# One group-scan kernel: the stack of high and low rows built by DMAs from SBUF to SBUF instead of by TensorE transposes, with the job table placed anew

## The chip, the cores and the metric

The kernel runs on one core of one Trainium2 chip. The metric is the device time of one execution in microseconds, taken as the median of several runs; lower is better. TensorE is called PE here, VectorE DVE, ScalarE ACT, GpSimd POOL, SyncE SP.

## The reference

The input is 32 sequences of 64 tokens with 1024 channels, all in fp32. Two adapted layers are applied with residuals:

```
u  = x W + (x A[id1]) B[id1]                      # per sequence a LoRA pair, rank 16
xp = u xproj^T -> dt_in (32), B (16), C (16)
dt = softplus(dt_in dtproj^T + b)
h_t = exp(dt A) * h_{t-1} + dt * u * B_t          # 1024 channels x 16 states, 64 steps
x1 = x + sum_n h_t[n] C_t[n] + D * u
h2 = x1 W2^T + bias + lora2[id2](x1)              # folded into the router and expert product
out = x1 + sum_e gate_e(h2) * 4 * (h2 A_e^T) B_e^T    # top 2 of 4 experts, softmax over them
```

## The kernel before, in words

The work is cut into 8 groups (`GROUPS`) of 4 sequences, T = 256 tokens. A group is run as 8 steps j, one for each 128 channels, and a step as 4 units (`UNITS`): unit `un` is half = un // 2 of the 16 states and p = un % 2 of the tokens. There are 256 units in all. A unit is a pipeline over four engines. PE computes `dBx` = B * dt * u in PSUM by 4 matmuls with 96 contraction rows (`b_times_dtx`); DVE scans it with the decays `dA` that ACT has made (8 ACTIVATEs a half step, `decays`); POOL multiplies the states by `Cb` into `hC`; and three units later PE sums the 8 states by accumulating transposes into a bank `yp` (`sum_states`), to which `Du` = D * u is added.

The 96 rows of `dBx`'s weights are the diagonals `Bd` (32 tokens by 32, three times: high, high and low part of B) and its moving operand is `stacked`: for each of the 8 blocks of 32 tokens, the high, the low and again the high part of dtx = dt * u, with tokens on the partitions. In the kernel before it is made in five steps for each j: POOL makes `dtx` (channels on partitions, `make_dtx`), ACT rounds it and writes it twice into `HL` (`make_high`), POOL subtracts (`make_low`), PE transposes 8 blocks 128 x 96 into PSUM in two jobs named `stack`, and ACT copies each of the two into `stacked`. `stacked` has two buffers, one for even and one for odd j.

Everything else is cut into jobs (`cond` is the first product x W, `xT`, `xr`, `xproj`, `dtz`, `Bst` lead to the next group's operands, `x1T`, `mid`, `mid2`, `gate`, `gm`, `out` finish the previous group). The table `JOBS` says by hand behind which unit (j, un) PE issues them and into which PSUM bank: "A" and "B" are the banks `jb`, "Y" is the bank `yp[j % 2]`, which stands empty until the sum of that step starts at (j, 3). `FIRST`, `SIXTH` and `FINAL` are the tables of groups 0, 6 and 7. ACT and DVE follow the same table, each job in the same or, for the names in `LATE_ON_ACT` and `LATE_ON_DVE`, in the next unit. `DTX`, `HIGH`, `LOW`, `DU` and `DIAGONALS` place the other pieces. Each engine runs its list in order; semaphores tie them. A unit's `dBx` may not start before the scan two units back is done, since `dBx` has two buffers.

SP issues nearly all DMAs, in order, and waits in its own list: `load_W` (1 MB for each `cond`), `spread_c` (C of the next group to all partitions), `load_xres`, the adapters' rows (`load_lora_a`, `load_lora_b`, `load_lora2`), `put_c` and `store`. The four diagonals of a group (`b_diagonals`, L742) are DVE products of `Bhl` and `diag`, both in SBUF.

Ahead of group 0 stands a prologue: W is loaded, split into high and low parts and written to `W_scratch`, group 0's `cond` products run in between, and `times_W2` folds W2 into the router and the experts. In it SP loads the parameters in program order, and ACT waits for `s_par` behind `cond` 1 before it makes `negA`.

Of the kernel before, what the change touches and what calls it, by code (L numbers as in the profile page):

```python
# [1198 lines left out]
```

## Time and profile before

| | |
|---|---|
| median of 3 runs | 965.89 us (965.32 to 972.38) |
| profiled execution | 970.02 us |
| its span, first to last instruction | 968.3 us |
| granted TensorE clock, mean of the span | 0.975 |
| PE busy | 870.6 us, 90% |
| DVE busy | 763.4 us, 79% |
| POOL busy | 729.5 us, 75% |
| ACT busy | 699.0 us, 72% |
| first and last `hC` product start | 98.9 and 944.4 us |

The busy shares are means over a prologue of some 95 us, eight groups and an end of some 24 us. Groups 1 to 6 repeat the same pattern every 107.0 us. A busy PE includes the time in which a matmul drains behind the next, so busy sums run a little above the time that PE's order really takes.

### The profile page before, as it was taken

The page shows a single profiled execution, that of the slowest core. Times are in us where ns is not written, and L with a number is a line of the kernel's source. Part 1 is how long each engine was busy: PE and PEld are TensorE (multiplying, and loading weights), DVE is VectorE, ACT ScalarE, POOL GpSimd, SP SyncE. Part 2 cuts the span into 40 slices and gives each one's busy share as a digit, 9 for nine tenths or more (in the row PEclk, how much of TensorE's full clock was granted, in tenths as well). Part 3 has the DMA queues.
Part 4 walks back from the last instruction along what each step waited for, and adds up shares of the span by engine and source line. Part 5 has one row for each costly group of instructions (what it writes and reads, how often), then busy time and mean ns, then how long its engine had stood idle before and what let it go on. Part 6 is the DMA issues. An engine that isn't in the chain of part 4 may idle for free.

```text
span 968.3 us, 19503 instructions
## 1 busy us (share of the span) xinstructions
PE 870.6 (90%) x6712; PEld 781.0 (81%) x6712; DVE 763.4 (79%) x613; ACT 699.0 (72%) x1594; POOL 729.5 (75%) x407
## 2 busy tenths in 40 slices
PE   4885899989998999989998999999998999888885
PEld 3663799879977999779987999789878998677672
DVE  2123967898889979897889979897889878898992
ACT  3225866887768877787768877788777977788850
POOL 1001877798788988698788988699778988899891
PEclk9898999999999999999999999999999999999997
DMA  9975366254441545354351645355442433131011
GB/s 263 289 262 193 85 180 201 80 175 153 103 165 54 205 129 167 99 185 143 90 178 52 207 123 172 100 185 154 117 148 96 158 105 88 35 104 34 28 39 44
DMA packets 128975, 130.36 MB, mean 135 GB/s; under 512 B 81129, under 2 KB 109801, under 8 KB 120686
## 3 DMA queue, kind: packets, MB, share of 16 engines
q1 hardware_dynamic: 114766, 108.79, 36.8%
q10 hardware_dynamic: 14112, 20.32, 6.3%
q8 instruction: 56, 0.92, 0.4%
q14 instruction: 41, 0.34, 0.1%
HBM read 112.16 MB, written 16.91 MB: 133 GB/s over the span
## 4 chain that ended last, share of the span: by engine, by line
PE 67%; POOL 10%; issue 6%; ACT 6%; DVE 6%; SPq 4%; DMA 1%; POOLq 0%; ACTq 0%; DVEq 0%
PE jb L918 29%; PE yp L1084 17%; PE dBx L918 10%; POOL hC L498 8%; PE yp L922 5%; ACT dA L544 3%; PE jb L922 3%; DVE h L890 3%; PE yp L918 2%; SPq L308 2%; DVE Bd L742 1%; ACT stacked L570 1%; DMA bias_sb<-in_L_cond_base_bias 1%; PE yp L1089 1%; SPq L307 1%
## 5 line engine op out<-in xcount | busy, mean ns | idle before, releaser
L498 POOL TENSOR_TENSOR hC<-h,Cb 128x1024 f32<-128x1024 f32 x256 | 618.4, 2425 | 91.9 <-DVE h L890 88.5
L890 DVE TENSOR_TENSOR_SCAN h<-dA,dBx 128x1024 f32<-128x1024 f32 x256 | 583.0, 2281 | 96.2 <-PE dBx L918 66.3
L544 ACT ACTIVATE dA<-dt,negA 128x252 f32<-128x252 f32 x1024 | 424.7, 494 | 9.2 <-DVE h L890 9.0
L1084 PE MATMUL yp<-ident,hC 128*128 128x128 f32 x2048 | 268.8, 274 | 10.1 <-DVE Bhl L821 4.6
L1084 PEld LDWEIGHTS yp<-ident,hC 128*128 128x128 f32 x2048 | 232.5, 142 | 12.6 <-POOL hC L498 7.9
L918 PE MATMUL jb<-xT,Wst 128*128 128x256 f32 x1536 | 234.7, 296 | 7.1 <-DVE Wst L846 5.2
L918 PEld LDWEIGHTS jb<-xT,Wst 128*128 128x128 f32 x1536 | 199.5, 193 | 16.8 <-issue 13.1
L918 PE MATMUL dBx<-Bd,stacked 96*128 96x256 f32 x1024 | 184.0, 302 | 30.5 <-DVE h L890 9.6
L918 PEld LDWEIGHTS dBx<-Bd,stacked 96*128 96x128 f32 x1024 | 142.9, 192 | 44.7 <-issue 42.4
L570 ACT ACTIVATE stacked<-yp 96x512 fp32r<-96x512 f32 x111 | 65.6, 591 | 111.4 <-PE yp L922 111.2
L477 POOL TENSOR_TENSOR dtx<-dt,u 128x256 f32<-128x256 f32 x64 | 55.5, 868 | 86.5 <-DVE dt L728 78.0
L481 POOL TENSOR_TENSOR HL<-dtx,HL 128x256 f32<-128x256 f32 x64 | 61.2, 956 | 36.6 <-ACT HL L534 36.5
L922 PE MATMUL yp<-ident,HL 128*96 128x128 f32 x444 | 67.7, 275 | 5.4 <-ACT stacked L570 3.9
L742 DVE TENSOR_TENSOR Bd<-Bhl,diag 96x1024 fp32r<-96x1024 f32 x32 | 62.7, 1966 | 0.0
L922 PEld LDWEIGHTS yp<-ident,HL 128*96 128x96 f32 x444 | 49.2, 127 | 10.0 <-ACT stacked L570 6.3
L534 ACT ACTIVATE HL<-dtx 128x512 fp32r<-128x512 f32 x64 | 39.7, 620 | 21.0 <-PE yp L922 17.7
L806 DVE TENSOR_TENSOR xT<-jb,xT 128x512 fp32r<-128x512 f32 x32 | 22.0, 688 | 30.4 <-ACT xT L575 30.3
L575 ACT ACTIVATE xT<-jb 128x512 fp32r<-128x512 f32 x32 | 18.9, 592 | 30.7 <-PE jb L922 30.5
L918 PE MATMUL jb<-low,GB 128*128 128x256 f32 x128 | 38.2, 380 | 0.5 <-DMA GB<-in_L_cond_lora_B 0.5
L1089 PE MATMUL yp<-ident,Du 128*128 128x128 f32 x128 | 35.2, 275 | 0.0
L918 PE MATMUL jb<-G,x1T 128*128 128x132 f32 x256 | 33.0, 276 | 0.7 <-ACT x1T L573 0.7
L922 PEld LDWEIGHTS jb<-ident,xin 128*128 128x128 f32 x128 | 15.3, 155 | 22.2 <-issue 12.3
(131 smaller groups left out, 721.7 us busy)
## 6 DMA issues: line engine op xcount, KB each, us to landing
Wst<-W_scratch SPq DMA_DIRECT2D x56, 1024.0 KB, 5.1
Cb<-c_scratch SPq DMA_DIRECT2D x32, 512.0 KB, 4.9
W_scratch<-Wst ACTq DMA_DIRECT2D x8, 1024.0 KB, 6.6
xres<-in_x SPq DMA_DIRECT2D x64, 128.0 KB, 4.5
out<-obuf SPq DMA_DIRECT2D x32, 256.0 KB, 2.0
xin<-in_x ACTq DMA_DIRECT2D x28, 256.0 KB, 6.2
GB<-in_L_cond_lora_B SPq DMA_DIRECT2D x64, 64.0 KB, 2.0
Cb<-in_L_cond_W ACTq DMA_DIRECT2D x4, 512.0 KB, 7.4
```

The costliest lines, as they stand in the source:

```text
L477: pool.tensor_tensor(dtx[:, :], dt[:, i % NDT, :], u[:, i % K, :], ALU.mult).then_inc(dtx_made, 1)
L481: pool.tensor_tensor(HL[:, :, 1, :].bitcast(fp32), dtx[:, :].rearrange("p (q t) -> p q t", q=NQ), HL[:, :, 0, :].bitcast(fp32), ALU.subtra ...
L498: pool.tensor_tensor(hC[:, un % NHC, :].rearrange("p (n b t) -> p b n t", n=HS, b=2), h[:, un % NH, :].rearrange("p (b n t) -> p b n t", n ...
L534: act.activation(HL[:, :, 0:3:2, :], dtx[:, :].rearrange("p (q t) -> p q t", q=NQ).unsqueeze(2).to_broadcast([P, NQ, 2, Q]), ACT.Copy).the ...
L544: act.activation(dA[:, half % NDA, :].rearrange("p (b n t) -> p b n t", b=GB_, n=HS)[:, :, n, 1:STEPS], dt[:, j % NDT, :].rearrange("p (b ...
L570: act.activation(stacked[0:ROWS, i // 2 % 2, NQ // 2 * half:NQ // 2 * (half + 1), :].rearrange("p q d -> p (q d)"), psum[0:ROWS, :], ACT.C ...
L742: dve.tensor_tensor(Bd[0:ROWS, NQ // 2 * p:NQ // 2 * (p + 1), HS * half:HS * (half + 1), :], Bhl[0:ROWS, NQ // 2 * p:NQ // 2 * (p + 1), HS ...
L890: dve.tensor_tensor_scan(h[:, un % NH, :], dA[:, half % NDA, UNIT * p:UNIT * (p + 1)], dBx[un % 2][:, :], 0.0, ALU.mult, ALU.add).then_inc ...
L918: return pe.matmul(o, lhsT, rhs, start=start, stop=stop, **kw)
L922: return pe.matmul(o, in_, ident[first:first + n, first:first + n], is_transpose=True, start=True, stop=True)
L1084: last = pe.matmul(y, hC[:, un % NHC, P * n:P * (n + 1)], ident[:, :], is_transpose=True, start=un == 0 and n == 0, stop=False, skip_group ...
L1089: last = pe.matmul(y, Du[:, j % 4, P * p:P * (p + 1)], ident[:, :], is_transpose=True, start=False, stop=True, skip_group_check=True)
```

## The change

`dtx` itself, channels on partitions, is transposed on PE by two 128 x 128 transposes a step into one bank. ACT rounds the 128 x 256 result into `HL` (high) and DVE subtracts it from the bank (low). SP then lays out `stacked` by twelve DMAs a step from SBUF to SBUF, each of 32 partitions and 1 KB a partition: the blocks of 32 tokens go to partitions 0 to 31 (high), 32 to 63 (low) and 64 to 95 (high). `dBx` waits for the DMAs' semaphore, once a step. `make_high`, `make_low`, the eight 128 x 96 transposes and the two copies of a step are gone. `stack` for step i is a single job, and the tables move it and nearly every other job. `HL` has one buffer: ACT writes it again only when the previous step's DMAs have landed.

The diagonals read `Bst`'s rows in PSUM instead of `Bhl` in SBUF. The seven or eight `load_W` of a group go from SP's to ACT's list. The gating chain of small DVE operations is cut into five pieces over three units, with waits only where an operand needs them. In the prologue `cond` 1 starts ahead of `xr`, the adapters are loaded first, `negA` is made behind the `cond` loop, `load_lora_a(1)` stands ahead of the last four chunks of W2, and the first unit no longer waits for the taking of `times_W2`'s result.

```diff
-    (0, 0): [stack(2), job("stack", 3, "B"), job("cond", 1, "A", (4, 7))],
...
-    (7, 3): [job("cond", 1, "A", (0, 4), 2)],
+    (0, 0): [job("A2T", 0, "Y"), job("cond", 1, "A", (3, 5))],
+    (0, 1): [job("cond", 1, "A", (5, 8))],
+    (0, 2): [job("stack", 2, "Y"), job("x1T", 0, "B"), job("cond", 2, "A", (0, 6)), job("x1T", 1, "B")],
...
+    (1, 1): [job("cond", 3, "A", (0, 3)), job("stack", 3, "Y"), job("x1T", 3, "B")],
...
+    (2, 1): [job("cond", 4, "A", (1, 2)), job("stack", 4, "Y"), job("mid", 0, "B", (3, 6))],
...
+    (3, 3): [job("rank", 1, None), job("cond", 5, "A", (5, 8)), job("gate", 0, None), job("gate", 1, None)],
+    (4, 0): [job("stack", 5, "Y"), job("cond", 6, "A", (0, 4))],
+    (4, 1): [job("gm", 0, "B"), job("cond", 6, "A", (4, 6)), job("out", 0, "B")],
+    (4, 2): [job("stack", 6, "Y"), job("cond", 6, "A", (6, 7)), job("out", 1, "B"), job("GAs", 0, None)],
...
+    (5, 2): [job("stack", 7, "Y"), job("xproj", 0, "A", (0, 4)), job("xT", 1, "B")],
...
+    (6, 1): [job("xT", 2, "A"), job("Bst", 0, "B"), job("xT", 3, "Y")],
+    (6, 2): [job("dtz", 4, "A")],
...
+    (7, 0): [job("cond", 0, "A", (0, 3), 2), job("xr", 0, "Y", (0, 4)), job("xr", 0, "Y", (4, 8)), job("stack", 8, "Y")],
+    (7, 1): [job("cond", 0, "A", (3, 7), 2), job("dtz", 5, "Y")],
+    (7, 2): [job("stack", 9, "Y"), job("cond", 0, "A", (7, 8), 2)],
+    (7, 3): [job("cond", 1, "A", (0, 3), 2)],
...
+LATE_ON_ACT = {"A2T", "Bst", "GAs", "cond", "dtz", "gate", "gm", "h2T", "mid2", "stack", "x1T", "xT", "xr"}
+LATE_ON_DVE = {"GAs", "cond", "dtz", "gate", "rank"}
+DTX = {(0, 0): 2, (0, 1): 3, (1, 3): 4, (2, 1): 5, (3, 3): 6, (4, 2): 7, (6, 2): 8, (7, 1): 9}
+DU = {(0, 1): 2, (1, 3): 3, (2, 2): 4, (3, 0): 5, (4, 1): 6, (5, 0): 7, (7, 0): 8, (7, 1): 9}
...
+ADAPTERS = {(3, 3): 0, (4, 0): 1, (5, 3): 2}
+DIAGONALS = {(0, 0): 2, (0, 1): 3, (7, 0): 0, (7, 1): 1}
...
-        HL = sb("HL", [P, NQ, 3, Q], fr)
-        stacked = sb("stacked", [P, 2, NQ, P], fr)
+        HL = sb("HL", [P, 2, 2, P], fr)
+        stacked = sb("stacked", [P, 2, NQ // 2, 2, P], fr)
...
+        def load_W(eng, g, o):
+
+            eng.wait_ge(full["cond"], K * g + o - 1)
+            eng.dma_start(W_chunk(o), W_scratch[o]).then_inc(W_in[o % 2], 16)
...
+            def stack_dtx(G, i):
+                t = K * G + i
+                wait_alone(sp_e, sp_passed, taken["stack"], t + 1, dBx_full, UNITS * (t - 1))
+                for third, h_ in enumerate((0, 1, 0)):
+                    for a in range(NQ // 2):
+                        sp_e.dma_start(stacked[Q * third:Q * (third + 1), i % 2, a, :, :].bitcast(fp32),
+                                       HL[Q * a:Q * (a + 1), h_, :, :].bitcast(fp32)).then_inc(stacked_in[i % 2], 16)
...
+            load_lora_a(1)
             for k in range(4, K):
                 sp_e.wait_ge(gt_full, k - 3)
                 sp_e.dma_start(W2c[k % 4], W2[P * k:P * (k + 1), :]).then_inc(s_W2[k % 4], 16)
             put_c(0)
+            stack_dtx(0, 0)
             for un in range(UNITS):
                 spread_c(0, un)
+            stack_dtx(0, 1)
...
-            def make_low(G, i):
-                pool.wait_ge(hi_made, K * G + i + 1)
-                pool.tensor_tensor(HL[:, :, 1, :].bitcast(fp32), dtx[:, :].rearrange("p (q t) -> p q t", q=NQ),
-                                   HL[:, :, 0, :].bitcast(fp32), ALU.subtract).then_inc(lo_made, 1)
...
-            def make_high(G, i):
-                t = K * G + i
-                act.wait_ge(dtx_made, t + 1)
-                wait(act, full["stack"], 2 * t)
-                act.activation(HL[:, :, 0:3:2, :], dtx[:, :].rearrange("p (q t) -> p q t", q=NQ).unsqueeze(2).to_broadcast([P, NQ, 2, Q]),
-                               ACT.Copy).then_inc(hi_made, 1)
...
                 if name == "stack":
-                    half = i % 2
-                    wait(act, dBx_full, UNITS * (K * g + i // 2 - 2) + 3 + half)
-                    act.activation(stacked[0:ROWS, i // 2 % 2, NQ // 2 * half:NQ // 2 * (half + 1), :].rearrange("p q d -> p (q d)"),
-                                   psum[0:ROWS, :], ACT.Copy).then_inc(taken[name], 1)
+                    if K * g + i:
+                        act.wait_ge(stacked_in[(i + 1) % 2], 192 * ((K * g + i + 1) // 2))
+                    act.activation(HL[:, 0, :, :].rearrange("p q d -> p (q d)"), psum[:, 0:2 * P], ACT.Copy).then_inc(hi_made, 1)
...
+                if name == "stack":
+                    dve.wait_ge(hi_made, K * g + i + 1)
+                    dve.tensor_tensor(HL[:, 1, :, :].rearrange("p q d -> p (q d)"), psum[:, 0:2 * P],
+                                      HL[:, 0, :, :].bitcast(fp32).rearrange("p q d -> p (q d)"), ALU.subtract).then_inc(taken[name], 1)
...
+                            if name == "cond" and i + 2 < K:
+                                load_W(act, g, i + 2)
+                            elif name == "cond" and g + 1 < GROUPS:
+                                load_W(act, g + 1, i + 2 - K)
...
+                rows = jb["AB".index(BANK_OF_B) if G else 0][0:ROWS, 0:NQ * R].rearrange("p (q n) -> p q n", q=NQ)
                 dve.tensor_tensor(
                     Bd[0:ROWS, NQ // 2 * p:NQ // 2 * (p + 1), HS * half:HS * (half + 1), :],
-                    Bhl[0:ROWS, NQ // 2 * p:NQ // 2 * (p + 1), HS * half:HS * (half + 1)].bitcast(fp32).unsqueeze(3).to_broadcast(of),
+                    rows[:, NQ // 2 * p:NQ // 2 * (p + 1), HS * half:HS * (half + 1)].unsqueeze(3).to_broadcast(of),
...
                 elif name == "stack":
-                    pe.wait_ge(lo_made, K * g + i // 2 + 1)
-                    for a in range(NQ // 2):
-                        part = HL[:, NQ // 2 * (i % 2) + a, :, :].bitcast(fp32).rearrange("p h t -> p (h t)")
-                        last = tr(psum[0:ROWS, P * a:P * (a + 1)], part, P)
+                    pe.wait_ge(dtx_made, K * g + i + 1)
+                    for a in range(2):
+                        last = tr(psum[:, P * a:P * (a + 1)], dtx[:, P * a:P * (a + 1)], P)
...
-                if half == 0:
-                    wait_alone(pe, pe_passed, taken["stack"], 2 * t + p + 1)
+                if t == 0 and un == 1:
+                    wait_alone(pe, pe_passed, taken["dtz"], 2)
+                if un == 0:
+                    wait_alone(pe, pe_passed, stacked_in[j % 2], 192 * (t // 2 + 1))
```

## Rows read from the trace of the kernel before

**Rows 1.** The page's first part: busy time, share and instructions of each engine.

```profile
PE 870.6 (90%) x6712; PEld 781.0 (81%) x6712; DVE 763.4 (79%) x613; ACT 699.0 (72%) x1594; POOL 729.5 (75%) x407
```

**Rows 2.** Windows by stretch: busy time (instructions), granted clock, DMA share, GB/s.

```profile
95.00:205.00 110.00, 99.81 (x793) 94.10 (x794) 86.29 (x57) 82.31 (x189) 85.47 (x46) 0.97 0.45 130
...
328.30:399.60 71.30, 70.69 (x562) 63.90 (x560) 57.92 (x50) 55.17 (x127) 59.13 (x32) 1.00 0.47 141
399.60:435.30 35.70, 30.00 (x246) 28.05 (x246) 35.01 (x24) 29.83 (x69) 30.93 (x16) 1.00 0.41 139
...
633.00:740.00 107.00, 103.18 (x831) 94.60 (x830) 92.89 (x75) 84.97 (x196) 91.38 (x49) 1.00 0.46 141
...
863.00:900.00 37.00, 31.51 (x269) 29.05 (x268) 32.12 (x33) 32.49 (x76) 35.84 (x21) 1.00 0.14 26
```

**Rows 3.** The chain that ended last, 440 to 450: start, us, what.

```profile
440.17 0.45 PE yp L922 x4
...
448.71 0.46 PE dBx L918 x4
449.17 0.88 PE yp L1084 x8
```

**Rows 4.** Groups of instructions over the span: busy us, mean ns; idle before.

```profile
L890 DVE TENSOR_TENSOR_SCAN h<-dA,dBx 128x1024 f32<-128x1024 f32 x256 | 583.0, 2281 | 96.2 <-PE dBx L918 66.3 <-ACT dA L544 17.9 <-POOL hC L498 10.8
...
L922 PE MATMUL yp<-ident,HL 128*96 128x128 f32 x444 | 67.7, 275 | 5.4 <-ACT stacked L570 3.9 <-DVE x L734 1.5
L570 ACT ACTIVATE stacked<-yp 96x512 fp32r<-96x512 f32 x111 | 65.6, 591 | 111.4 <-PE yp L922 111.2
L742 DVE TENSOR_TENSOR Bd<-Bhl,diag 96x1024 fp32r<-96x1024 f32 x32 | 62.7, 1966 | 0.0
L481 POOL TENSOR_TENSOR HL<-dtx,HL 128x256 f32<-128x256 f32 x64 | 61.2, 956 | 36.6 <-ACT HL L534 36.5
...
L734 DVE TENSOR_TENSOR x<-yp,xres 128x256 f32<-128x256 f32 x64 | 26.1, 408 | 4.0 <-PE yp L1089 3.7
```

**Rows 5.** The diagonals' line (ns min/median/max), then two rows of the timeline.

```profile
L742 DVE TENSOR_TENSOR Bd<-Bhl,diag x32: 1209/1753/4858, 83.8 to 859.4; 96x1024 fp32r<-96x1024 f32 x32
...
421.04 1.74 POOL L481 TENSOR_TENSOR HL<-dtx,HL 128x256 f32<-128x256 f32 x1
...
430.13 4.86 DVE L742 TENSOR_TENSOR Bd<-Bhl,diag 96x1024 fp32r<-96x1024 f32 x1
```

**Rows 6.** SP's queue in the timeline; last, the page's DMA issues (us to landing).

```profile
98.62 9.72 SPq L308 DMA_DIRECT2D GB<-in_L_cond_lora_B  x8
...
454.17 6.50 SPq L308 DMA_DIRECT2D GA<-in_L_cond_lora_A  x4
...
477.72 4.03 SPq L308 DMA_DIRECT2D B2g<-in_L_cond_lora_B_w  x4
...
515.22 1.37 SPq L342 DMA_DIRECT2D c_scratch<-BC  x4
...
out<-obuf SPq DMA_DIRECT2D x32, 256.0 KB, 2.0
x1T<-in_L_cond_base_weight SPq DMA_DIRECT2D x4, 512.0 KB, 5.7
```

**Rows 7.** The prologue's timeline: start, us, what [idle before <- releaser].

```profile
28.29 3.75 PE L918 MATMUL jb<-xT,GAs 128*128 128x256 f32 x16 [7.63 <-DVE GAs L800]
...
49.96 1.05 SPq L386 DMA_DIRECT2D x1T<-in_L_cond_base_weight  x2
50.23 0.31 ACT L663 ACTIVATE negA<-negA 128x128 f32<-128x128 f32 x1 [8.95 <-DMA bias_sb<-in_L_cond_base_bias]
...
53.39 4.51 PE L918 MATMUL jb<-xT,Wst 128*128 128x256 f32 x24 [4.72 <-DVE Wst L846]
...
82.79 0.69 DVE L728 SCALAR_TENSOR_TENSOR dt<-jb,dt 128x512 f32<-128x512 f32 x1 [3.16 <-ACT dt L522]
...
95.29 1.19 PE L918 MATMUL dBx<-Bd,stacked 96*128 96x256 f32 x4 [5.03 <-ACT obuf L686]
```

More of the change, by code:

```diff
@@ L364, in _ @@
                 load_x(sp_e, 0, i)
+            sp_e.wait_ge(s_idx, 32)
+            load_lora_a(0)
+            load_lora_b(0)
             sp_e.dma_start(F_n[0:EM, :], expA.rearrange("e r d -> (e r) d")).then_inc(s_F, 16)
@@ L367, in _ @@
             sp_e.dma_start(b_raw, dtproj_b.rearrange("(o n) -> o n", o=1)).then_inc(s_b, 16)
-            sp_e.wait_ge(s_idx, 32)
-            load_lora_a(0)
+            for k in range(2):
+                sp_e.dma_start(W2c[k], W2[P * k:P * (k + 1), :]).then_inc(s_W2[k], 16)
             sp_e.dma_start(negA[:, :, :], A_log.rearrange("(k p) n -> p k n", p=P)).then_inc(s_par, 16)
-            load_lora_b(0)
             for e in range(E):
@@ L486, in _ @@
                 make_dtx(0, i)
-                make_low(0, i)
             def body(G, par):
@@ L503, in body @@
                             make_dtx(G, DTX[j, un])
-                        if (j, un) in LOW and not (final and LOW[j, un] >= K):
-                            make_low(G, LOW[j, un])
             groups(pool, body)
@@ L661, in _ @@
                             .then_inc(set_taken, 1)
-                    act.wait_ge(s_par, 48)
-                    act.activation(negA[:, :, :], negA[:, :, :], ACT.Exp).then_inc(s_neg, 1)
-                    act.wait_ge(s_neg, 1)
-                    act.mul(negA[:, :, :], negA[:, :, :], -1.0).then_inc(s_neg, 1)
+                if o == 5:
+                    for i in range(4):
+                        load_x(act, 1, i)
                 if o == 3:
@@ L708, in body @@
                                 job(name, i, g, psum)
-                        if (j, un) in HIGH and not (last and HIGH[j, un] >= K):
-                            make_high(G, HIGH[j, un])
                         if (j, un) in DU and not (last and DU[j, un] >= K):
                             make_Du(G, DU[j, un])
-            for i in range(4):
-                load_x(act, 1, i)
             groups(act, body)
@@ L767, in gating @@
                 rank, chosen = kept[:, 64:72], kept[:, 72:80]
-                if not second:
-                    logits = mids[:, :, EM:EM + E]
+                logits = mids[:, :, EM:EM + E]
+                other, own = logits.unsqueeze(2).to_broadcast(pairs), te(5).unsqueeze(3).to_broadcast(pairs)
+                by_expert = chosen.rearrange("p (a e) -> p a e", a=TT)
+                if piece:
+                    linked()
+                if piece == 0:
                     top = gate[:, 2, 0:TT]
@@ L872, in _ @@
             job("Bst", 0, 0, 0, jb[0])
-            for un in range(UNITS):
+            b_diagonals(0, 0)
+            job("stack", 0, 0, 0, jb[1])
+            b_diagonals(0, 1)
+            job("stack", 1, 0, 0, jb[1])
+            for un in range(2, UNITS):
                 b_diagonals(0, un)
-            job("dtz", 1, 0, 0, jb[1])
+            job("dtz", 1, 0, 0, set_bank(2))
             def body(G, par):
@@ L907, in _ @@
             job("mid2", 0, G, G % 2, jb[0])
-            job("gate", 0, G, G % 2, jb[0])
+            for i in range(2):
+                job("rank", i, G, G % 2, jb[0])
+            for i in range(2):
+                job("gate", i, G, G % 2, jb[0])
             for i in range(4):
```

225 lines of the change are left out of this document (112 added, 113 removed).

## The prediction

> **What bounds the kernel now.** I began with the page's first part [rows 1]: PE is busy 90% of the span, DVE 79%, POOL 75%, ACT 72%. These are means over unlike stages, so the next view was the windows [rows 2]. A steady group takes 107.0 us, and it falls into two parts. For 71.3 us PE is busy 70.7 of them, DVE only 57.9: PE's order of work is the bound. In the 35.7 us around the turn of the group (steps 7 and 0) DVE is busy 35.0 and PE 30.0: there DVE is the bound. The chain that ended last says the same for the long part: it is piece after piece of PE, with 0.46 us for the four `dBx` matmuls, 0.88 us for eight summing transposes, and 0.45 us for four 128 x 96 transposes of `HL` [rows 3]. So one 0.45 us piece there is worth 0.45 us of time. Group 7 has less PE work; in its windows POOL is busy 35.8 us of 37.0 [rows 2].
>
> **PE's part of the change.** The transposes of a step fall from eight to two. The 128 x 128 ones of the sums cost 0.88 / 8 = 0.11 us, the 128 x 96 ones 0.45 / 4 = 0.11 us [rows 3]: 0.90 us becomes 0.22, so 0.68 us less a step, 5.4 us a group. In the table before, five of the eight steps' stacks lie in the PE-bound part and three around the turn. PE's busy time of a group goes from 103.2 [rows 2] to 97.8 us. The mean of 275 ns for such a transpose [rows 4] is not the price, since it holds the drain that overlaps the next one. The waits of PE for `stacked` (3.9 us over the run for L922, [rows 4]) also go with it, but they are small.
>
> **DVE's part.** It gains a subtraction of 128 x 256 from PSUM a step. The residual (L734) has that shape and also one operand in PSUM: 0.41 us [rows 4], so 3.3 us a group. It loses time in the diagonals. Their 32 cost 62.7 us, a mean of 1.97 [rows 4], yet one has been done in 1.21 us, and the longest took 4.86 [rows 5]. POOL suffers too: a subtraction on `HL` took 1.74 us beside one, against a mean of 0.96 [rows 4, 5]. I read this as the two engines shutting each other out while DVE has both operands in SBUF. With `Bst`'s rows in PSUM one operand leaves SBUF. Nothing in this trace shows a diagonal so placed; the bounds are 1.97 us (no change) and 1.21 us. I take 1.21, since the residual, whose operands lie the new way, has no such spread about its mean of 0.41 us. That is 0.76 us x 4 = 3.0 us a group, all around the turn, where DVE is the bound. The Trainium skill (SBUF — State Buffer, section Who interferes with whom) says that a DVE instruction with two SBUF inputs contends with GpSimd's reads and one with at most one SBUF input does not; by it 1.21 us would hold, by the bare row 1.97 us and 3 us less gain a group.
>
> The gating's split removes some waits of 0.03 us and spreads 3 us of small operations over three units; I cost it at nothing, under PE's bound.
>
> **POOL and ACT.** POOL loses `make_low`: 61.2 us over the run [rows 4], 7.6 us a group. ACT loses two copies of 0.59 us a step [rows 4] and its write of `HL` becomes half as wide; it gains the issue of eight W loads a group, at some 0.34 us each by the row of four issues in 1.37 us [rows 6], 2.7 us. ACT comes from 85 busy us of 107 [rows 2] to about 76. Neither engine is the bound of a steady group, so this is worth nothing there; what hides it is PE's order. In group 7 POOL is the bound in part, and I count half of its 7.6 us.
>
> **SP and the DMAs.** The new stack waits behind this chain: two transposes (0.22), ACT's copy (some 0.4), DVE's subtraction behind the running scan (2.3 us [rows 4], and 0.4), twelve issues and one landing. An issue is bounded by 0.34 us (`put_c`, four in 1.37) and 1.2 us (`load_lora_b`, eight in 9.72, with their register loads) [rows 6]. `put_c` is nearest: it too leaves SBUF with few partitions. Twelve are 4.1 us. Landing is bounded by 2.0 us (`out<-obuf`, from SBUF) and 5.7 us (512 KB into SBUF) [rows 6]; I take 2.0, as the pieces are 32 KB. From the start of the unit that holds the job: about 3.3 us to DVE's end, 4.1, 2.0, so 9.4 us. The shortest notice in the new table is four units (stack 5 at (4, 0), stack 8 at (7, 0)), 4 x 3.15 = 12.6 us. It fits by 3 us. SP's list also holds the adapters: `load_lora_a` 6.5 us at (3, 3) and `load_lora2` some 8 us (4.03 for one half) at (4, 0), just ahead of stack 5 [rows 6]. SP is freed by stack 4's issue, some 5 us after unit (2, 3); 14.5 us later it is at (4, 1), about when DVE has stack 5 ready. It fits with about 2 us. SP's total for a group is 96 x 0.34 = 33 us new and some 30 us old (6.5 + 8 + 9.7 for the adapters, 1.4 for `put_c`, and twelve loads of C and x at some 0.4): 63 of 107.
>
> **A steady group.** If the parts stay as they are cut, the PE-bound one gets 5 x 0.68 = 3.4 us shorter; the turn has DVE at 35.0 - 3.0 + 3 x 0.41 = 33.2 us, 1.8 us shorter. That makes 101.8. If the new table balances PE and DVE over the whole group, PE's 97.8 us with some stalls makes 98.5 us. DVE's total (92.9 - 3.0 + 3.3 = 93.2) is below both. I take 101.0: 6.0 us less, in six groups 36 us. Group 0 (110 us window at 99.8 PE busy, [rows 2]) gets 5 us, group 7 gets 4.
>
> **The prologue.** Three waits of PE are touched [rows 7]. It stood 7.63 us ahead of `xr` for the split of the adapters; now `cond` 1 (some 3 us) runs in it. It stood 4.72 us at 53.4 because ACT had waited 8.95 us for the last parameter; `negA` is made behind the loop now, and this goes. Some 8 us in all; what is late next is W2. Chunk 4 was issued at 49.96 [rows 7]; now `load_lora_a(1)` stands ahead of it, 6.5 us, and a landing of 5.7 [rows 6]: 62 us, where PE, 8 us earlier than now, would want it at 60. I take 5.5 us of the 8. At the end of the prologue dt is ready at 83.5 (82.79 + 0.69), yet the first `dBx` waits until 95.29, 5.03 us of it for the copies that no longer stand before it [rows 7]. The new stack needs from 83.5: `dtx` 0.7, transposes 0.4, ACT behind four decays 2.0, DVE 0.4, twelve issues 4.1, landing 2.0: 93.1. That is 2 us earlier, but SP's other DMAs are dense there; I take 0.5. Prologue: 6 us, between 0 and 11.
>
> **Sum.** 36 + 5 + 4 + 6 = 51 us. The profiled execution took 970.0 us, so 919 by it; the median of the runs is 965.9, 4.1 below, so **915 us**. Bounds: with 98.5 us a group, 6, 5 and 11 for the rest, 73 us less: 893. With 101.8 plus the 3 us of diagonals that gain nothing, 2.2 us less a group, 3 each for groups 0 and 7 and nothing in the prologue, only 19 us less: 947. All bad ends together are unlikely; the forecast's own range is 893 to 930.
>
> **The rivals.**
>
> *Stacks that come late.* SP reaches stack 5 behind 14.5 us of adapter loads, and stack 8 has four units' notice. If issues cost 0.6 us instead of 0.34 (3.1 us more for twelve), both are late by 0 to 3 us, and PE stands. ACT's write of `HL` for stack 9 waits for stack 8's landing, and DVE, whose list holds its subtraction, behind it. Price: about 3 us a group over seven groups, 21 us: 936 us. For it: a busy SP [rows 6]. Against: 63 of 107 us.
>
> *DVE and ACT in lockstep.* DVE now waits in its own order for ACT's half of each stack. Were that 0.7 us for each of 8 steps, 5 us a group, PE's gain would be given back: T = 106, 959 us, no change. Against: ACT stood 111 us in 86 waits for PE in the row of L570 [rows 4], so it is ahead of the others at these jobs.
>
> *SP's queue becomes the bound (slower).* Its place is SP's list in every group: 96 issues more. At p us each a group needs 96 p + 30 us, and above p = 0.8 that is more than 107. With the 1.2 us of `load_lora_b` [rows 6] it is 145 us a group, 38 more in eight groups: some 1270 us; at 0.85 us, 112 a group, about 1000. For it: that row. Against: `put_c` at 0.34. The Trainium skill (DMA: Bandwidth & Descriptors, Anatomy of one DMA) gives each DMA a fixed cost of about 2 us beside its bytes, and calls transfers under 64 KB descriptor-dominated; were that cost paid in series, an estimate of 24 us a step would make the kernel some 1500 us long. The trace speaks against the series, not against the latency: eight DMAs of 64 KB were issued within 9.72 us [rows 6].
>
> **How the numbers follow.** The forecast has 0.72, late stacks 0.13, lockstep 0.07, SP's queue 0.08. A change under 1% (9.7 us) can't be told from none. Faster by more: 0.85; within: 0.07; slower: 0.08. The range runs from the forecast's low end to over the late stacks: 893 to 945.
>
> **What would show it.** Right: windows of a steady group at 99 to 102 us, `yp<-dtx` transposes near 0.11 us in the chain, L742's successor at 1.2 us with hardly a spread, the HL rows gone from POOL, `dBx` waits on `stacked_in` of a few us in total. Wrong: PE idle ahead of `dBx` with a DMA into `stacked` as releaser; SP issues of the twelve over 0.4 us; DVE idle ahead of the subtraction behind ACT; a first `dBx` after 90 us. What would break the sum most is a step time set by the DMAs.

## The result and the profile after

The changed kernel takes **1116.8 us** (median of four runs, 1114.2 to 1120.3), the kernel before 966.1: a ratio of 1.155, 95% interval 1.149 to 1.160. The forecast was 915 us, with 945 as its high end. It is slower by 151 us where I expected 51 less. (Ratios here leave disturbed runs out on both sides; where a kernel's ratio and its median seem to differ, the ratio counts.) The profiled execution took 1120.3 us, its span is 1118.5. The page after, its busy time and the shares of the chain that ended last:

```profile
PE 901.1 (81%) x6328; PEld 800.4 (72%) x6328; DVE 759.3 (68%) x677; ACT 629.4 (56%) x1467; POOL 659.1 (59%) x343
...
SPq 32%; PE 29%; DMA 13%; issue 9%; POOL 7%; DVE 6%; ACT 3%; POOLq 0%; ACTq 0%; DVEq 0%
```

Every engine has fallen in share against [rows 1], PE too (90 to 81%), though it is busy 30 us longer. The first name in the chain is SPq, SyncE issuing DMAs. No compute engine bounds this kernel. The groups over the span say who stands behind it (after "|": busy time, mean ns; then idle time just before):

```profile
L1113 PE MATMUL yp<-ident,hC 128*128 128x128 f32 x2048 | 290.0, 288 | 72.2 <-DVE HL L822 66.1
...
L568 ACT ACTIVATE HL<-yp 128x256 fp32r<-128x256 f32 x62 | 23.3, 376 | 181.3 <-DMA stacked<-HL 147.3
L822 DVE TENSOR_TENSOR HL<-yp,HL 128x256 fp32r<-128x256 f32 x62 | 25.8, 417 | 127.3 <-ACT HL L568 127.3
...
L737 DVE TENSOR_TENSOR x<-yp,xres 128x256 f32<-128x256 f32 x64 | 26.5, 414 | 45.3 <-DMA xres<-in_x 36.8
...
L746 DVE TENSOR_TENSOR Bd<-jb,diag 96x1024 fp32r<-96x1024 f32 x32 | 38.2, 1197 | 0.0
```

Read from the second row down: ACT waits 147 us for the DMAs that still read `HL`, DVE waits 127 us for ACT, and PE waits 66 us for DVE, since its sums go into the bank of the stack's job. The last row is the diagonals' of [rows 4]: 1.20 us where they took 1.97. The DMAs' own line, in ns (min/median/max), and the time from issue to landing in us:

```profile
L360 SPq DMA_DIRECT2D stacked<-HL x768: 507/591/1902, 81.6 to 1075.8; - x192
...
DMA to landing us min/median/max: 1.7/1.9/7.2
```

The landing is what I took (2.0 us). The issue is not: 0.59 us at the median where I took 0.34. One stack in the timeline, stack 5 and the beginning of stack 6:

```profile
549.23 7.52 SPq L360 DMA_DIRECT2D stacked<-HL  x12
...
558.13 0.38 ACT L568 ACTIVATE HL<-yp 128x256 fp32r<-128x256 f32 x1 [6.99 <-DMA stacked<-HL]
...
558.54 0.42 DVE L822 TENSOR_TENSOR HL<-yp,HL 128x256 fp32r<-128x256 f32 x1 [6.28 <-ACT HL L568]
...
559.12 1.94 PE L1113 MATMUL yp<-ident,hC 128*128 128x128 f32 x8 [5.91 <-DVE HL L822]
559.14 8.30 SPq L360 DMA_DIRECT2D stacked<-HL  x12
```

These rows show how the loss arises. Twelve issues last 7.5 us (0.63 each, and 8.3 for the next twelve); `HL` is free 1.4 us after the last. Stack 6's transposes were done long before (PE waits for DVE, not for itself), but ACT can't overwrite `HL`, and ACT, DVE and PE each take their work in order, so all three stand 6 to 7 us. The eight sums then ran 1.94 us instead of 1.04: the window 558 to 563 has a granted clock of 0.50, and in the one from 553 to 558 PE was busy 0.21 us.

ACT's waits for landing come to some 20 us a steady group. About 7 stand ahead of stack 6 and 4 ahead of stack 9, each two units behind the stack before it. The other 9 stand ahead of the stacks of steps 2 to 4, three and four units behind theirs. There the start of the twelve matters as well. For stacks 2 and 3 it comes 1.3 to 4.1 us after DVE's half is ready, because SP first waits until the buffer of `stacked` is free (SP's own waits: us in total, times, longest):

```profile
SPq L242 <- PE dBx L945: 39.7, 22, 4.0
```

A window of one group, from its first diagonal to the next group's (columns as in [rows 2]):

```profile
595.70:725.40 129.70, 104.83 (x786) 94.54 (x785) 93.18 (x83) 76.46 (x179) 82.08 (x41) 0.95 0.48 141
```

A group takes 129.7 us against 107.0 in [rows 2]. Busy times are about as forecast (DVE 93.2, ACT 76.5). PE's is not: 104.8 here, and 107.4 in the mean of five steady groups, at a granted clock of 0.90 to 0.95. Run 1 below, without the DMAs, has 100.3 at 0.97:

```profile
sum 649.40, PE 536.80 PEld 484.95 DVE 465.27 ACT 382.09 POOL 410.13; mean PE 107.36 PEld 96.99 DVE 93.05 ACT 76.42 POOL 82.03
sum 529.90, PE 501.63 PEld 459.16 DVE 464.41 ACT 382.67 POOL 411.35; mean PE 100.33 PEld 91.83 DVE 92.88 ACT 76.53 POOL 82.27
```

The first row is this kernel's sum and mean over its groups from 205.8 to 855.2 us, the second run 1's from 191.0 to 720.9. So of the 24 us that the DMAs add to a group, PE stands for 17 and is busy for 7 more, at the lower clock.

### The profile page after: what moved, and what is told of

Read it like the earlier page. It is cut to its first block, busy times and chain, and to the rows that moved or that the text cites. A ratio compares the mean times of both kernels' runs of the same rounds, so it can differ in the third digit from the quotient of the medians.

```text
span 1118.5 us, 18818 instructions
## 1 busy us (share of the span) xinstructions
PE 901.1 (81%) x6328; PEld 800.4 (72%) x6328; DVE 759.3 (68%) x677; ACT 629.4 (56%) x1467; POOL 659.1 (59%) x343
## 4 chain that ended last, share of the span: by engine, by line
SPq 32%; PE 29%; DMA 13%; issue 9%; POOL 7%; DVE 6%; ACT 3%; POOLq 0%; ACTq 0%; DVEq 0%
SPq L360 25%; PE jb L945 14%; DMA stacked<-HL 8%; POOL hC L505 7%; PE yp L1113 6%; SPq L314 5%; PE yp L945 4%; PE dBx L945 3%; DVE h L914 3%; DMA xres<-in_x 2%; SPq L312 2%; PE jb L949 2%; DMA W_scratch<-Wst 1%; DVE HL L822 1%; ACT HL L568 1%
## 5 line engine op out<-in xcount | busy, mean ns | idle before, releaser
L1113 PE MATMUL yp<-ident,hC 128*128 128x128 f32 x2048 | 290.0, 288 | 72.2 <-DVE HL L822 66.1
L945 PE MATMUL jb<-xT,Wst 128*128 128x256 f32 x1536 | 257.7, 315 | 27.9 <-DVE dt L731 20.1
L945 PEld LDWEIGHTS jb<-xT,Wst 128*128 128x128 f32 x1536 | 219.9, 211 | 34.4 <-DVE dt L731 21.6
L568 ACT ACTIVATE HL<-yp 128x256 fp32r<-128x256 f32 x62 | 23.3, 376 | 181.3 <-DMA stacked<-HL 147.3
L822 DVE TENSOR_TENSOR HL<-yp,HL 128x256 fp32r<-128x256 f32 x62 | 25.8, 417 | 127.3 <-ACT HL L568 127.3
L737 DVE TENSOR_TENSOR x<-yp,xres 128x256 f32<-128x256 f32 x64 | 26.5, 414 | 45.3 <-DMA xres<-in_x 36.8
L949 PE MATMUL yp<-ident,dtx 128*128 128x128 f32 x124 | 25.7, 291 | 24.5 <-DVE dt L731 17.1
L746 DVE TENSOR_TENSOR Bd<-jb,diag 96x1024 fp32r<-96x1024 f32 x32 | 38.2, 1197 | 0.0
L570 ACT ACTIVATE x1T<-jb 128x512 f32<-128x512 f32 x32 | 19.0, 594 | 26.4 <-PE jb L949 26.4
L945 PEld LDWEIGHTS jb<-G,x1T 128*128 128x128 f32 x256 | 31.5, 194 | 2.0 <-ACT x1T L570 1.1
```

The source lines that it names most:

```text
L746: dve.tensor_tensor(Bd[0:ROWS, NQ // 2 * p:NQ // 2 * (p + 1), HS * half:HS * (half + 1), :], rows[:, NQ // 2 * p:NQ // 2 * (p + 1), HS * h ...
L822: dve.tensor_tensor(HL[:, 1, :, :].rearrange("p q d -> p (q d)"), psum[:, 0:2 * P], HL[:, 0, :, :].bitcast(fp32).rearrange("p q d -> p (q ...
L945: return pe.matmul(o, lhsT, rhs, start=start, stop=stop, **kw)
L949: return pe.matmul(o, in_, ident[first:first + n, first:first + n], is_transpose=True, start=True, stop=True)
L1113: last = pe.matmul(y, hC[:, un % NHC, P * n:P * (n + 1)], ident[:, :], is_transpose=True, start=un == 0 and n == 0, stop=False, skip_group ...
```

## The experiments

All ratios are to the kernel before in the same session; version N is the kernel of experiment N. Where two versions come from different sessions, their ratios are compared. Group periods are the time between the first diagonals (`Bd`) of successive groups; in the kernel before they are 104 to 111 us (two of them 110 and 111, so the pattern doesn't repeat at 107.0 every time), after 122 to 132.

**1. No DMAs of the stacks from the third on.** What is left out: the moving, so `dBx` is made from the first two stacks.

```diff
+                if t >= 2: return      # stack_dtx
-                        act.wait_ge(stacked_in[(i + 1) % 2], 192 * ((K * g + i + 1) // 2))
-                    wait_alone(pe, pe_passed, stacked_in[j % 2], 192 * (t // 2 + 1))
+                    wait_alone(pe, pe_passed, taken["stack"], t + 1)   # t >= 2
```

> Leaves out the twelve DMAs of every step but the first two of the run, so stacked keeps old contents; dBx waits for DVE's subtraction instead. Theory HOLD (one HL buffer: ACT may write the next high part only when the twelve DMAs of the step before have landed, 8 us of issues plus 2 us, and DVE and PE queue behind ACT) and rival SP LIST (the issues fill SP's own list): both say that the rest of the change is as forecast, so about 915 us. Rival PLACEMENT (the new job tables, the W loads on ACT's list or the later copies are slow by themselves): above 1050 us.

952.1 us, ratio 0.986 (0.979 to 0.993). The DMAs cost 165 us; without any of them the change is worth 14 us, not 51. The 915 us that both theories gave is missed by 37, and the placement rival (above 1050) is out. Groups take 105.8 us where I had forecast 101.0.

**2. Six of the twelve DMAs**, the other six left out (half of each stack is stale).

```diff
-                    for a in range(NQ // 2):
+                    for a in range(NQ // 2 if t < 2 else 2):
```

> Leaves out six of the twelve DMAs of each step from step 2 on (the blocks a = 2, 3 keep old contents); nothing else changes. HOLD: a stack's DMAs then take some 4 us of issues and 2 us of landing, 6 us, which is the distance of the two closest stacks (two units), so the waits nearly vanish: 920 to 945 us. SP LIST: the same range, since the list has 31 us less a group. PLACEMENT: no less than 1080 us.

980.0 us, ratio 1.015 (1.007 to 1.024), above the 920 to 945 of both theories; run 1 has already shown some 37 us of that to be no matter of the DMAs. An issue costs the same 0.591 us at the median, and ACT's wait for them falls from 155 to 52 us:

```profile
ACT HL L568 <- DMA stacked<-HL: 52.4, 19, 7.9
```

So the first six DMAs of a stack cost 28 us over the run and the second six 137. The price isn't in the issues as such; it rises steeply once they outlast the distance between stacks.

**3. Two buffers for `HL`.**

```diff
-        HL = sb("HL", [P, 2, 2, P], fr)
+        HL = sb("HL", [P, 2, 2, 2, P], fr)
```

> HL gets a second buffer, so that ACT waits for the DMAs of two steps back; all twelve DMAs stay. HOLD: ACT's waits for landing (155 us in the profile) fall under 20 us and the time comes to 930 to 970 us. SP LIST: the DMAs still take 8 us a step to issue and the later loads stand behind them; the stacks of steps 8 and 9 and the x rows come late just the same, 1060 to 1115 us.

1056.7 us, ratio 1.086 (1.075 to 1.097). ACT's wait for the DMAs is gone, as it must be, yet the time is far above the 930 to 970 of the theory HOLD. Three rows of the list of waits (us in total, times, longest), from an execution of 1059.0 us:

```profile
DVE x L737 <- DMA xres<-in_x: 48.4, 26, 6.4
PE dBx L945 <- DMA stacked<-HL: 38.7, 9, 6.8
POOL hC L505 <- DMA Cb<-c_scratch: 36.6, 11, 6.4
```

PE's wait for the stacks themselves is new. The residual's `x` and `C` were late before as well (36.8 and 35.5 us in the changed kernel). The hold of `HL` alone was worth 60 of the 165 us by the medians, 66 by the ratios. The rest I put down to SP's list, in which the loads stand behind 7.7 us of issues; no run has the second buffer and a short list.

**4. By way of device memory.** One store of `HL` (256 KB), three loads of 128 KB; nothing left out. `HL` is free when the store has landed.

```diff
-                for third, h_ in enumerate((0, 1, 0)):
-                    for a in range(NQ // 2): sp_e.dma_start(stacked[...a...], HL[...a...])
+                sp_e.dma_start(hl_scratch[i % 2], HL)
+                wait_alone(..., hl_out, 16 * (t + 1))
+                for third, h_ in enumerate((0, 1, 0)):
+                    sp_e.dma_start(stacked[Q * third:Q * (third + 1), i % 2], hl_scratch[i % 2, h_])
```

> The stack goes by way of device memory: one store of HL (256 KB) and three loads of 128 KB each that rearrange the blocks, four issues a step in place of twelve; HL is free when the store has landed. Everything else as in the changed kernel. HOLD: HL is held for one issue and one landing, 2.5 us, and stacked is ready about 2.5 + 1.5 + 3 = 7 us after DVE: 920 to 950 us. SP LIST: 4 issues a step, but SP stands some 2 us a step for the store: 930 to 960 us. If instead the landing of loads from device memory (5 us by the W rows) sets the step, PE waits at the four-unit stacks: about 990 us.

959.8 us, ratio 0.991 (0.987 to 0.995), at the upper end of SP LIST's range and above HOLD's. A stack needs two landings in series (2.4 and 2.6 us) and 256 KB more of traffic, and the kernel is 157 us faster for it. In the timeline:

```profile
597.76 0.36 SPq L360 DMA_DIRECT2D hl_scratch<-HL  x1
599.98 1.27 SPq L364 DMA_DIRECT2D stacked<-hl_scratch  x3
```

Four issues, 1.6 us of SP's time instead of 7.5. `HL` gains in a second way: its store stands ahead of SP's wait for a free buffer of `stacked`, where the twelve stood behind it. No run parts the two.

**5. Twelve DMAs with a quarter of the row** (256 bytes a partition, in two rows of 128; the rest of each row is left stale).

```diff
-                        sp_e.dma_start(stacked[..., i % 2, a, :, :], HL[..., h_, :, :])
+                        sp_e.dma_start(stacked[..., i % 2, a, :, 0:c], HL[..., h_, :, 0:c])   # c = P // 4
```

> The changed kernel, but from step 2 on each of the twelve DMAs moves 256 B a partition in two rows of 128 B in place of 1 KB in one (only the first 32 channels of each half are copied, the rest of stacked keeps old contents). Theory ISSUE (a price for each DMA on SP's sequencer, whatever it moves): the issues stay at 0.5 to 0.6 us and the time at 1080 to 1125 us. Rival BYTES (SP is held back by the transfer itself): the issues fall to some 0.35 us and the time to 990 to 1030 us.

1115.3 us, ratio 1.154 (1.148 to 1.160): no change at all for a quarter of the bytes, and the issue stays at 0.597 us. The cost is a price for each DMA, not for what it moves.

**6. Version 4 with stack 9 moved** from (7, 2), where bank Y still waits for `dtz` 5, to (0, 0) of the next group, and `A2T` to (0, 1).

```diff
-    (7, 2): [job("stack", 9, "Y"), job("cond", 0, "A", (7, 8), 2)],
+    (7, 2): [job("cond", 0, "A", (7, 8), 2)],
-    (0, 0): [job("A2T", 0, "Y"), job("cond", 1, "A", (3, 5))],
+    (0, 0): [job("stack", 1, "Y"), job("cond", 1, "A", (3, 5))],
```

> e4_by_DRAM with one job moved: step 1's stack from behind unit (7, 2), where it stands in the same bank right behind dtz 5 and PE waits for DVE's taking of that, to (0, 0) of the next group, and A2T from (0, 0) to (0, 1). Theory TURN (PE's waits of 2.4 us for dt and some more around the turn are what the forecast lacked): a group comes from 105 to 107 down to 102 to 104, 20 us less in all: about 940 us. Rival: the waits move to the next job in the same bank, the time stays at 955 to 960.

952.4 us, ratio 0.985 (0.980 to 0.990), 7 us less than version 4, with intervals that touch. It is neither the 940 us of the theory nor the 955 to 960 of the rival, and its groups take 104.6 to 109.7 us, not 102 to 104.

**7. Version 4 with the diagonals read from SBUF** (`Bhl`) as before the change.

```diff
-                    rows[:, NQ // 2 * p:..., HS * half:...].unsqueeze(3)
+                    Bhl[0:ROWS, NQ // 2 * p:..., HS * half:...].unsqueeze(3)
```

> e4_by_DRAM with one part undone: the diagonals read Bhl in SBUF again (ACT copies all 96 rows), the bank is held just as long. If POOL and DVE shut each other out, the diagonals go from 1.2 us back to 1.6 to 4.9 us and the turn gets 2 to 4 us longer a group: 975 to 990 us. If DVE has slack at the turn now: no change, 955 to 965.

970.4 us, ratio 1.006 (1.003 to 1.009), between the two expected ranges. The group of the diagonals beside version 4's 1.20 us:

```profile
L748 DVE TENSOR_TENSOR Bd<-Bhl,diag 96x1024 fp32r<-96x1024 f32 x32 | 46.2, 1446 | 0.0
```

Reading PSUM is worth 8 us of DVE here and 1.5% of the whole by the ratios, some 14 us. POOL is relieved too: it is busy 86.0 us a group here and 82.3 in version 4.

**8. The kernel before with only the new stack**, by way of device memory: old table of jobs, diagonals from SBUF, W on SP.

```diff
-    stack(2), job("stack", 3, "B")         # the old table, one of its pairs
+    stack(1)
-                        last = tr(psum[0:ROWS, P * a:P * (a + 1)], part, P)      # 4 of HL
+                        last = tr(psum[:, P * a:P * (a + 1)], dtx[:, P * a:P * (a + 1)], P)   # 2
```

> The kernel before with its own job tables, W loads on SP, diagonals from SBUF and old prologue; only the stack is new: two transposes a step, ACT's and DVE's halves, one store and three loads by way of device memory, placed at (j, 0) for most steps. PLACEMENT as the rest of the loss: this keeps the old turn, saves PE 0.68 us a step and gives 925 to 945 us. Rival: PE's saving is taken up by waits of PE for DVE's half of the stack before the next job of bank Y, 955 to 970 us.

1008.9 us, ratio 1.043 (1.040 to 1.047), 64 us above the theory's range and 39 above the rival's. Its waits:

```profile
PE dBx L921 <- DMA stacked<-hl_scratch: 53.9, 23, 18.2
```

In the new table version 4 shows 3.6 us of this wait. Half of the 53.9 us are two waits ahead of the first steady group, 9.2 us at the first `dBx` and 18.2 at 123.7 us; the first diagonal of the second group comes at 214.6 us, 20 later than in the kernel before. The next five groups take 111.5 to 114.0 us. The new table has several of the jobs two or three units earlier than I had put them in the old one, which fits, but this run differs from version 4 in four things at once and doesn't show that the table is the cause.

**9. The twelve split over two queues**, six by SP and six by ACT, at the end of the unit behind the job's.

```diff
+                            if name == "stack":      # ACT, end of the unit
+                                act.wait_ge(taken["stack"], K * g + i + 1)
+                                for third, h_ in enumerate((0, 1, 0)):
+                                    for a in (2, 3): act.dma_start(stacked[...a...], HL[...a...])
```

> The changed kernel with the twelve DMAs of a stack split: six are issued by SP as now, the other six by ACT, at the end of the unit behind the one that holds the job. Nothing is left out. Theory (the time is lost because one queue issues twelve in series at 0.62 us): each queue needs some 3.7 us, but ACT's six start up to a unit (3.15 us) later, and ACT has 3.7 us more a step, 29 a group, on 76: 985 to 1050 us. Rival (the DMA engines or the SBUF side serve these transfers one after the other, whichever queue they are on): an issue gets dearer, above 1 us, and the time stays at 1080 to 1120 us.

An earlier placing of ACT's six, ahead of its other work of that unit, deadlocks and has no time. This one: 1103.0 us, ratio 1.137 (1.132 to 1.143). Both expectations are half right. The price does not rise when two queues issue at once (333 of SP's 396 issues overlap one of ACT's, with the median of the others), so it is the issuing engine's, not the transfers':

```profile
L360 SPq DMA_DIRECT2D stacked<-HL x396: 507/592/2737, 81.7 to 1052.5; - x198
L722 ACTq DMA_DIRECT2D stacked<-HL x372: 514/614/1899, 102.7 to 1052.2; - x186
```

The time stayed nearly as it was all the same, though ACT's wait for the DMAs fell from 155 to 12 us. What took its place, as I read it, are ACT's own issues: the 372 take 240 us, and they stand inside its order of work. I had counted 29 us a group for them, on an engine with room. One block in the timeline, and the work behind it:

```profile
587.53 3.68 ACTq L722 DMA_DIRECT2D stacked<-HL  x4
591.31 0.51 ACT L533 ACTIVATE Du<-u,Dsb 128x256 f32<-128x256 f32 x1 [3.90 <-issue]
```

In the list of waits ACT's `Du`, `dt` and `dA` stand 48, 42 and 41 us at "issue" (time without a wait that the profile shows, here the DMAs ahead of them), and POOL's wait for the scans is 284 us, as long as in the changed kernel (296).

**10. Version 6 with the W loads on SP again.**

```diff
-                                load_W(act, g, i + 2)
+                                load_W(sp_e, g, i + 2)     # in SP's list, where the cond job ends
```

> The version by way of device memory with stack 9 moved to the turn's first unit (952 us), and the W loads moved back from ACT's queue to SP's. Nothing is left out. Theory (SP has room now, four issues a stack, and a wait of SP for a cond job's bank only delays loads that are early): within 0.5% of 952. Rival (W on SP holds back the stacks behind it, as in the old table by way of device memory at 1009): 960 to 975 us.

Ratio 1.000 (0.994 to 1.006), so 1.5% above version 6, give or take 0.8: the rival. SP waits for the bank of each `cond` job with the stacks queued behind it:

```profile
SPq L293 <- PE jb L948: 59.8, 24, 7.2
```

ACT's wait for the store of `HL` doubles with it, from 11.2 to 22.9 us. On ACT's queue these loads cost nothing that shows.

**11 to 13. Why a group takes 105.8 us and not 101.0.** In run 1 PE is busy 84.9 of the 85 us from 523 to 608; at the turn it is busy 2.46 of 5 us and the clock falls (columns as in [rows 2]):

```profile
603.00:608.00 5.00, 4.97 (x48) 4.59 (x47) 4.94 (x7) 4.92 (x13) 4.44 (x2) 1.00 0.26 85
608.00:613.00 5.00, 2.46 (x20) 2.01 (x18) 5.00 (x5) 4.07 (x10) 2.82 (x3) 0.91 0.01 3
613.00:618.00 5.00, 5.00 (x24) 5.00 (x25) 3.08 (x2) 1.39 (x4) 5.00 (x3) 0.50 0.00 0
```

One theory: the table leaves PE nothing in unit (6, 3), and 5 us at the granted clock of 0.50 follow; the other: DVE bounds the turn (5.00 of 5 in the middle window). Run 11 is version 6 and run 12 is run 1, both with `dtz` 4 and `xT` 3 moved a place and a piece of `cond` 0 at (6, 3); run 13 is version 6 with the `dBx` of (6, 3) issued three times.

```diff
-    (6, 1): [job("xT", 2, "A"), job("Bst", 0, "B"), job("xT", 3, "Y")],
-    (6, 2): [job("dtz", 4, "A")],
-    (6, 3): [],
+    (6, 1): [job("xT", 2, "A"), job("Bst", 0, "B"), job("dtz", 4, "Y")],
+    (6, 2): [job("xT", 3, "A")],
+    (6, 3): [job("cond", 0, "A", (0, 2), 2)],
...
-                for a in range(NQ // 2):
+                for a in list(range(NQ // 2)) * (3 if (j, un) == (6, 3) and G < GROUPS - 1 else 1):
```

> The version by way of device memory with stack 9 moved (952 us), and the jobs at the end of step 6 placed so that PE has work in unit (6, 3): dtz 4 into bank Y at (6, 1), xT 3 into bank A at (6, 2), and the first two slices of cond 0 at (6, 3). Nothing is left out. Theory (once a group PE stands 1.1 and 1.4 us around (6, 3), the clock is granted at 0.50 for the next 5 us, and this, not DVE, is why a group takes 105 and not 101 us): the clock stays at 1.00 there, a group takes 100.5 to 102.5, the whole 922 to 935 us. Rival (DVE bounds the turn: it is busy 35.1 of 37.9 us there): at most 1 us a group, 944 to 952.

> The changed kernel without the DMAs of the stacks from the third on (they are left out, so dBx is made from the first two), as the run that gave 952 us, and with the jobs at the end of step 6 placed as in the run without the gap at the turn. Theory (the rest of the miss, 37 us, is this gap and the half clock behind it): 918 to 930 us, which is what the forecast priced. Rival (DVE bounds the turn): 944 to 952.

> The version by way of device memory with stack 9 moved (952 us), and the four dBx matmuls of unit (6, 3) of each group but the last issued three times over, with the same result: 8 matmuls more, 1.3 us, at a place where PE otherwise stands. Nothing is left out. Theory (of the 4.8 us that a group takes longer than forecast, about half is matmuls run at the clock granted at 0.50 behind that stand of PE): with PE kept at work there the clock stays higher and a group takes 2 to 2.5 us less, the whole 935 to 942 us. Rival (the clock falls in any case because PE still waits 1.1 us ahead of these dBx, or DVE bounds the turn whatever PE does): 951 to 960 us.

Run 11: 949.4 us, ratio 0.977 (0.974 to 0.981). Run 12: 946.5 us, 0.973 (0.970 to 0.976), leaving out what run 1 does. Both land in the rival's range by their medians. By the ratios they are 0.8% below version 6 and 1.3% below run 1, some 8 and 13 us, so filling the place gains something, but not the 17 to 34 us of the theory. PE's wait for DVE's `dt` was only moved: 1.41 us ahead of `cond` 0 in run 1, in run 12 this, ahead of the sums of the unit before:

```profile
605.08 1.06 PE L1115 MATMUL yp<-ident,hC 128*128 128x128 f32 x8 [2.17 <-DVE dt L733]
```

Run 13: 953.7 us, 0.984 (0.977 to 0.991), also the rival's. Here the stretch has a clock of 1.00 where run 1 had 0.50, and against version 6 (0.985) nothing shows; PE still waits 1.4 us for DVE's `dt` ahead of `cond` 0:

```profile
608.00:613.00 5.00, 3.16 (x26) 2.71 (x25) 5.00 (x5) 4.07 (x10) 2.82 (x3) 1.00 0.01 2
613.00:618.00 5.00, 4.48 (x38) 4.28 (x38) 4.01 (x5) 2.30 (x7) 5.00 (x3) 1.00 0.00 0
```

A steady group of run 1, one of run 12 and one of run 13, the last two without a dip of the clock:

```profile
509.10:614.90 105.80, 100.20 (x781) 91.70 (x781) 92.87 (x84) 76.50 (x179) 82.32 (x41) 0.97 0.45 143
192.60:296.10 103.50, 98.12 (x788) 90.01 (x786) 92.84 (x83) 76.39 (x179) 82.06 (x40) 1.00 0.47 146
510.70:614.80 104.10, 98.79 (x791) 90.39 (x790) 92.86 (x84) 76.38 (x179) 82.39 (x41) 1.00 0.64 195
```

So the low clock is worth at most some 2 of the 4.8 us by which a group is too long. The rest is PE standing, 5.3 to 5.6 us in each of the three, where the forecast left 3.2 (101.0 less 97.8). In run 1 some 2.4 and 1.4 us of it are waits for DVE's `dt`:

```profile
PE yp L951 <- DVE dt L733: 17.9, 7, 3.3
PE jb L947 <- DVE dt L733: 8.8, 7, 1.4
```

The best kernel of the study is run 11, 2.3% faster than the kernel before.

## Why the prediction was wrong

**The price of an issue: the term that failed.** I bounded it by 0.34 and 1.2 us, took `put_c`'s end as nearest and named "0.34 us" and "4.1 us" for twelve. It is 0.59 us (median), 7.5 to 9.9 us for twelve as the timeline has them. `put_c` also leaves SBUF with few partitions, but it ends in device memory, as the store in version 4 does (0.38); no row of the trace before showed an issue from SBUF to SBUF. Per group the 96 issues are 60 us of SP, not 33.

**The test of fit: the step that failed worse.** I checked the stack's chain (9.4 us) against its notice (12.6 us) and wrote "it fits by 3 us". That asks when the data is wanted. It doesn't ask when `HL` is wanted back: two stacks stand only two units apart, 6.3 us, at (4, 0) and (4, 2) and at (7, 0) and (7, 2). Even at my own price, 4.1 us of issues and 2.0 of landing filled that distance; at 0.59 us the hold is 9 to 10. The close pairs are more than half of it, not all: ahead of stacks 3 and 4 the twelve start late, behind the wait for a free `stacked`. Run 2 shows the edge (six issues, 28 us), run 3 the share of the hold (60 to 66 of 165).

**The rival "stacks that come late" had the mechanism and not the size.** It had the issue at 0.6 us and ACT's write of `HL` with DVE behind it, but priced 3 us a group. With the DMAs a group took 129.7 us, without them 105.8: 24, of which 7 are PE's work at a lower clock. I had counted a delay of up to 3 us; three engines that take their work in order stood behind each, up to 7 us. "SP's queue becomes the bound" named 0.8 us as the point from which it decides, by SP's total; SP was the chain's first name at 0.59. Sums of a queue's work say when it can't keep up, not when it is late.

**The steady group, 101.0 us.** Even without the DMAs it is 105.8 (run 1), 4.8 us more in each of six groups, 29 of the 37 us by which run 1 misses 915. PE's work was priced right: in run 12's group with a clock of 1.00 it is busy 98.1 us against 97.8 forecast; in run 1, at 0.97, 100.3. What I had too small is the stalls: some 3 us, and they are 5 to 6. My turn was 33.2 us of DVE "where DVE is the bound"; but the new table's turn has PE waiting for DVE's `dt` whichever bank it is in (runs 11 and 12), and more matmuls in PE's gap bring nothing that shows (run 13). That DVE bounds this turn is argued from its 5.00 us of 5 in one window; no run makes DVE's part shorter. I had let the two parts of the group be balanced by the table; they aren't.

**The prologue, 6 us.** The first `dt` was ready at 78.7 us, 4.7 earlier than in [rows 7], so the two waits of PE did shrink. Then twelve issues stood on the path, and the next row is of the timeline of after:

```profile
81.56 7.57 SPq L360 DMA_DIRECT2D stacked<-HL  x12
...
90.77 1.19 PE L945 MATMUL dBx<-Bd,stacked 96*128 96x256 f32 x4 [8.89 <-issue]
```

It began 4.5 us before that of [rows 7], yet with stack 1 behind another 7.5 us of issues the first product of POOL came only 2.5 us earlier.

**What was right.** Diagonals from PSUM: 1.19 to 1.22 us against 1.21 forecast, worth some 14 us (run 7). The Trainium skill (SBUF — State Buffer, Who interferes with whom) says that a DVE instruction with one SBUF input doesn't contend with GpSimd; the trace agrees, with a longest of 1.22 us where the form with both inputs in SBUF had 4.86. DVE's subtraction: 0.417 us (0.41). The landing: 1.9 us (2.0). POOL and ACT relieved: busy 82.0 and 76.4 us a group where they were 91.4 and 85.0. W's issues on ACT cost nothing that shows, and moving them back costs 1.5% (run 10). The lockstep of ACT and DVE that I priced at 5 us a group isn't there by itself: in run 1 DVE waits 23 us for ACT's half over the whole run. Of the Trainium skill's fixed 2 us a DMA (DMA: Bandwidth & Descriptors, Anatomy of one DMA, a section on DMAs issued by GpSimd; these are issued by SP and ACT) I had said that it isn't paid in series; that holds, the issues overlap the landings of 1.9 us. What is paid in series is the 0.6 us of the issuing engine.

**What stays open.** Why an issue from SBUF to SBUF costs 0.59 us where one to or from device memory costs 0.34 to 0.43; partitions, destination and distance of the rows weren't told apart, only bytes (run 5) and the queue (run 9) were excluded. How much of version 4's gain is the fewer issues and how much the store's earlier start isn't shown. And run 8's 1009 us is explained only in part: 1.5% for the diagonals and 1.5% for W by runs 7 and 10, the rest I take for its late stacks, without a run that moves these alone.

## What to carry to other kernels

Before replacing compute by many small DMAs, sum issues x price and hold it against the shortest distance between two uses of the **source** buffer, not only against the time until the data is wanted, and add what the queue waits for ahead of the first issue. The price is paid in series on one engine, so a way through device memory with four issues can be cheaper than twelve direct ones, though its landings stand in series. Look for what is queued in order behind the release of that buffer: each engine in that chain stands as long as the first. And price a low clock next to an idle stretch by a group that has the stretch and no dip: here it was 2 us of 4.8 at most at the turn, and 7 of the 24 us that the DMAs cost a group.

## What the runs showed of the hardware

An issue from SBUF to SBUF of 32 partitions costs 0.51 us at least and 0.59 at the median with 1 KB a partition, 0.53 and 0.60 with 256 bytes (run 5), 0.61 at the median on ACT (run 9), six or twelve in a row. SP and ACT issued at the same time without slowing each other (run 9). In version 4's list an issue to device memory costs 0.38 and one from it 0.43. The issues on ACT stand in its order of work: six took 4.0 us at the median, and for some 50 of the 240 us that all of them took ACT was computing at the same time (run 9).
